# Two gate and up units of the first tile computed ahead of the first flag, as fp32 products

## The reference

```python
# attn: three-tap convolutions, norm, linear attention with rotation, gate, MLP of 1024
x = x + dwconv(x); shortcut = x; xn = ln(x)
act_res = silu(xn @ actp_w + actp_b)
xi = silu(dwconv(xn @ in_w + in_b))
...
x = shortcut + attn * act_res @ out_w + out_b
...
# ffn: ternary weights (-1, 0, 1), scaled per row
h = silu((xn @ w1.T) * w1_s) * ((xn @ w2.T) * w2_s)     # 256 -> 1024: gate and up
h = gelu((h @ h1.T) * h1_s); h = gelu((h @ h2.T) * h2_s)
return (h @ w3.T) * w3_s
```

## Time and profile before

| | us |
|---|---|
| median of 3 runs (lowest, highest) | 1061.14 (1061.04, 1061.63) |
| the profiled execution | 1058.51 |
| its span, first to last instruction | 1056.7 |
| TensorE busy in the span | 1015.6 (96%) |
| VectorE, ScalarE, POOL busy | 760.4 (72%), 602.3 (57%), 237.4 (22%) |

### The profile page before, as it was taken

How to read it: one execution, slowest core, us unless ns; L and a number is a source line. 1 busy time by engine, 2 the same in 40 slices (tenths; PEclk the granted TensorE clock), 3 DMA queues, 4 the chain that set the end, 5 groups by cost and what they waited for, 6 DMA issues and landing times. The chain is left out here.

```text
span 1056.7 us, 17178 instructions
## 1 busy us (share of the span) xinstructions
PE 1015.6 (96%) x6628; PEld 907.1 (86%) x6628; DVE 760.4 (72%) x964; ACT 602.3 (57%) x875; POOL 237.4 (22%) x214
## 2 busy tenths in 40 slices
PE   3999999999999999999999999999999999999998
PEld 3778777888877778888888989989999999999998
DVE  6874689534548579988888466966878967776664
ACT  4788667676444364565555535556556654665444
POOL 3454255224305111111110120231200211101100
PEclk9999999999999999999999999999999999999999
DMA  8989614966784635524312673234493423222310
GB/s 308 408 252 387 201 61 153 330 206 209 282 285 162 195 119 199 180 81 142 118 60 81 228 271 118 81 100 143 155 381 148 152 81 121 91 75 83 113 41 22
DMA packets 68258, 180.15 MB, mean 170 GB/s; under 512 B 5024, under 2 KB 26144, under 8 KB 64544
## 3 DMA queue, kind: packets, MB, share of 16 engines
q1 hardware_dynamic: 68176, 179.03, 48.9%
HBM read 121.34 MB, written 66.06 MB: 177 GB/s over the span
## 5 line engine op out<-in xcount | busy, mean ns | idle before, releaser
L2278 PE MATMUL pr<-xp_hi,wb 128*128 128x256 f32 x1344 | 320.2, 282 | 1.3 <-DVE u L2012 1.1
L2278 PE MATMUL pr<-xp_lo,wb 128*128 128x256 f32 x1344 | 319.6, 281 | 0.0
L2278 PEld LDWEIGHTS pr<-xp_hi,wb 128*128 128x128 f32 x1344 | 255.3, 190 | 3.2 <-issue 3.2
L2278 PEld LDWEIGHTS pr<-xp_lo,wb 128*128 128x128 f32 x1344 | 255.8, 190 | 0.0
L2278 PE MATMUL pr<-u_hi,ring 128*128 128x512 f32 x256 | 102.3, 400 | 3.0 <-issue 1.1
L2278 PE MATMUL pr<-u_lo,ring 128*128 128x512 f32 x256 | 100.0, 391 | 0.0
L1426 ACT CAST xp_hi<-tf 128x1024 fp32r<-128x1024 f32 x48 | 50.2, 1046 | 57.3 <-PE pr L2278 19.9
L1056 POOL TENSOR_TENSOR ot<-ot,yg 128x512 f32<-128x512 f32 x14 | 25.2, 1805 | 244.5 <-DVE ot L2057 244.5
L2466 PE MATMUL pr<-wf_hi,h_hi 128*128 128x256 f32 x256 | 75.5, 295 | 0.6 <-DVE h_lo L1865 0.6
L2006 DVE TENSOR_TENSOR xp_lo<-tf,xp_hi 128x1024 fp32r<-128x1024 f32 x48 | 60.8, 1266 | 20.2 <-ACT xp_hi L1426 20.1
L2466 PE MATMUL pr<-wf_lo,h_hi 128*128 128x256 f32 x256 | 72.1, 281 | 0.0
(11 more groups left out here) (236 smaller groups left out, 2521.7 us busy)
## 6 DMA issues: line engine op xcount, KB each, us to landing
ring<-w_s SPq DMA_DIRECT2D x42, 512.0 KB, 7.3
uf<-h_s SPq DMA_DIRECT2D x16, 1024.0 KB, 5.0
wb<-s_s SPq DMA_DIRECT2D x8, 1024.0 KB, 9.7
wb<-w_s SPq DMA_DIRECT2D x6, 1024.0 KB, 10.9
vw<-v_s SPq DMA_DIRECT2D x8, 514.0 KB, 6.9
xt<-x SPq DMA_DIRECT2D x8, 512.0 KB, 6.0
xn_s<-xh SPq DMA_DIRECT2D x8, 512.0 KB, 9.0
stage<-w_gated SPq DMA_DIRECT2D x2, 2048.0 KB, 13.4
```

Source lines behind the costliest of these rows:

```text
L2278: return e.matmul(bank, w.bitcast(dt), v_.bitcast(dt), start=first, stop=last, skip_group_check=True)
```

## The change

The table gets a place `early` ahead of step -1 with units 0 and 1; `after_back2` of step -1 loses two. The four sums of these units (gate and up, m = 0 and 1) are computed in `opening` as plain fp32 products, straight from the staged piece 0 and `xh[0]`, without a split and without a flag: eight products of 512 columns, two chunks each. One stands before `norm_tokens(0)`, six between it and `norm_back(0)`, one after it. Their silu (ScalarE), gate (VectorE) and the high and low part of `u` for m = 0 move into the opening lists of those engines. The offsets and the bit sum move to `kv_bank`, so that the three banks are free; three quarters of the offsets go ahead of the transposes of tile 1. The ring is filled with pieces 1 to 6 (`filled` counts the fills of a slot). Two half checks no longer stand behind gates 0 and 1 but ahead of the loop. Unit 2 and 3 now stand at `first`, and so on.

```diff
-FRONT_ROOM = [(("p", P1_STEPS[0], "first"), 2, 1), (("p", P1_STEPS[0], "after_a1"), 1, 1),
+FRONT_ROOM = [(("p", P1_STEPS[0], "early"), 2, 0), (("p", P1_STEPS[0], "first"), 2, 1), (("p", P1_STEPS[0], "after_a1"), 1, 1),
               (("p", P1_STEPS[0], "after_a2"), 1, 1),
-              (("p", P1_STEPS[0], "after_back1"), 2, 1), (("p", P1_STEPS[0], "after_back2"), 2, 0)] + \
+              (("p", P1_STEPS[0], "after_back1"), 2, 1), (("p", P1_STEPS[0], "after_back2"), 0, 0)] + \
...
+EARLY = len(FRONT["p", P1_STEPS[0], "early"])
+def filled(piece):
+    return 16 * (piece // RING + int(piece % RING > 0))
@@ SyncE
-                for piece in range(RING):
+                for piece in range(EARLY // 2, EARLY // 2 + RING):
                     sp.wait_ge(staged(piece), 16)
-                    sp.dma_start(ring[:, piece, :].bitcast(F32), stage(piece)).then_inc(s["w_in"][piece], 16)
+                    sp.dma_start(ring[:, piece % RING, :].bitcast(F32), stage(piece)).then_inc(s["w_in"][piece % RING], 16)
...
-                if piece == RING:
+                if piece == RING + 1:
                     sp.wait_ge(s["w_kept"], 16)
...
-            sp.wait_ge(s["gate_mm"], 1)
+            sp.wait_ge(s["gate_mm"], EARLY + 1)
@@ POOL, ahead of the loop over the steps
+            pool.wait_ge(s["up_mm"], EARLY)
+            low_of_u(0)
@@ ScalarE
             def high_of_u(m):
                 e.wait_ge(s["gated"], m + 1)
+                if m < EARLY:
+                    e.wait_ge(s["checked"], FIRST_LAYER + 2)
                 e.copy(u1_hi[:, m, :], full1[:, m % 2, :]).then_inc(s["u_hi"], 1)
...
+            def silu_early(m):
+                e.wait_ge(s["gate_mm"], m + 1)
+                e.activation(silu1[:, m, :], front_bank[bank_use(m) % 3], ACT.Silu, scale=par("w1_s", m)) \
+                    .then_inc(s["silu_d"], 1)
...
             conv1_centre(1)
+            silu_early(0)
             apply_norm(0)
             apply_xn(2)
             high_of_norm(0)
+            silu_early(1)
             copy_xn(2)
             apply_xn(3)
             xi_out(0)
             act_out(0)
+            high_of_u(0)
@@ VectorE
+            def gate_early(m):
+                e.wait_ge(s["up_mm"], m + 1)
+                e.wait_ge(s["silu_d"], m + 1)
+                e.scalar_tensor_tensor(out=full1[:, m, :], in0=front_bank[(bank_use(m) + 1) % 3], scalar=par("w2_s", m),
+                                       in1=silu1[:, m, :], op0=ALU.mult, op1=ALU.mult).then_inc(s["gated"], 1)
...
             check_staged(range(1, 3))
+            gate_early(0)
             low_of_norm(0)
...
-            set_flag(0, front_bank[0][0:1, 0:1])
+            set_flag(0, kv_bank[0:1, 8:9])
+            gate_early(1)
             check_staged(range(4, 6))
             norm_moments(1)
             check_staged(range(6, 7))
+            for m in range(EARLY):
+                check_half(m)
@@ TensorE
+            def early(m, layer, k):
+                if m == 0 and layer == 0 and k == 0:
+                    e.wait_ge(staged(0), 16)
+                    e.wait_ge(s["xh_w"], 1)
+                use = bank_use(m) + layer
+                bank_read(use)
+                w = stage(0).rearrange("p (m w k n) -> p m w k n", m=2, w=2, k=KC)
+                last = e.matmul(front_bank[use % 3], w[:, m, layer, k, :], mid(xh[0])[:, k, :],
+                                start=(k == 0), stop=(k == KC - 1))
+                if k == KC - 1:
+                    last.then_inc(s[("gate_mm", "up_mm")[layer]], 1)
...
             def opening():
                 a_channels(0)
+                offsets_of_weights(0, 1, 2)
                 a_channels(1)
-                offsets_of_weights()
+                offsets_of_weights(3)
+                early(0, 0, 0)
                 norm_tokens(0)
+                early(0, 0, 1)
+                for layer, m in ((1, 0), (0, 1)):
+                    for k in range(KC):
+                        early(m, layer, k)
+                early(1, 1, 0)
                 norm_back(0)
+                early(1, 1, 1)
                 a_channels(2)
                 in_proj(0)
                 e.wait_ge(s["biased"], 1)
-                sum_bits(0, front_bank[0][0:1, 0:1])
+                sum_bits(0, kv_bank[0:1, 8:9])
```

## The result

The changed kernel takes 1062.45 us (median), the kernel before beside it 1061.01: a ratio of 1.0019, 95% interval 1.0010 to 1.0028, so 1.1 to 3.0 us slower. The forecast was 1059.7. The profiled execution took 1063.18 us, span 1061.4, mean granted clock 0.991 (before: 1058.51, 1056.7, 0.998).

The account below looks back on a forecast made before the run. TensorE was taken as the bound nearly everywhere, with VectorE beside it before the second flag. Opening 0, 1.4 us saved before the second flag, nothing given back later: median 1061.14 to 1059.7 us, range 1057.2 to 1062.2.

Parts of the forecast that it names:

- The price of the products: Opening, TensorE: one fp32 product of 512 columns costs 0.86 us at the higher clock level, 1.72 at the lower.
- the offsets into their gap: Opening, TensorE: twelve of sixteen offset instructions, 2.56 us, move into a gap of 2.53 us; cost about 0.05 us.
- `norm_back(0)` under its cover: Opening, TensorE: it ends at 28.0 us, without cost because ScalarE reads it only at 29.15; cover 1.1 us.
- `pb_lo` late: Sign of being wrong in the opening: VectorE's `pb_lo` starts later than the expected 30.2 us.
- products at 0.43 behind the hole: Sign of being wrong on the clock: TensorE products 0.43 us each after the new hole ahead of unit 4.
- From the first flag to the second: Stretch between the flags: TensorE loses 3.7 us of work, VectorE 0.74; hidden unit at 62.35 us, 1.4 us saved.
- gate 2 at 44.2: VectorE between the flags: gate 2 starts at 44.2 us, where VectorE has won 1.2 us and TensorE 4.3.
- 0 for the opening: Sum of the forecast: the opening, up to the first flag, neither saves nor costs time.
- u_lo(0) come after its other work: POOL: the added wait and `u_lo(0)` stand behind its other work; no cost was put down.
- the input projection starts at 31.5 as now: End of the opening, TensorE: the projection waits for `pb_lo` and starts at 31.5 us, unchanged.
- at the higher level: TensorE's input projection runs at the higher clock level from its start and ends some 0.6 us sooner.
- the clock falls in the new hole: Rival, chance 0.08: ahead of unit 4 TensorE idles 2.9 us, units 4 and 5 run at 0.43; 1061.5 us.

Follow-up runs that it names:

- e2: The changed kernel with `u_lo(0)` moved ahead of the inverse deviation of tile 1 on POOL; ratio to the kernel before 1.0004 [0.9991, 1.0016].
- e7: The changed kernel with both reorderings, `u_lo(0)` first on POOL and `gate_early(0)` between VectorE's two checks; 1059.58 us for 1060.88 before, ratio 0.9992.
- e8: e7 with `silu_early(1)` ahead of `apply_xn(2)`, `gate_early(1)` ahead of `pb_lo`, and half checks one behind each gate again; ratio to the kernel before 1.0009.
- e9: e8 plus five dummy fp32 products around the second bit sum, three ahead and two behind; ratio to the kernel before 1.0009 [0.9996, 1.0022].
- e11: e10 plus dummy fp32 products, read by nobody, around the second bit sum; ratio to the kernel before 0.9988 [0.9979, 0.9997].
- e3: The changed kernel with eight dummy products in the opening's holes, five ahead of tile 2's transposes and three behind; ratio to the kernel before 1.0012.
- e4: The changed kernel with `gate_early(0)` moved between VectorE's two staged checks; ratio to the kernel before 0.9998 [0.9986, 1.0009].
- e12: e11 with three dummy products around the second bit sum, two ahead and one behind, in place of five; 1059.36 us for 1061.09 before, ratio 0.9982.
- e6: The changed kernel with eight dummy fp32 products, read by nobody, between units 3 and 4; 1062.21 us, ratio to the kernel before 1.0005.
- e5: The kernel before, unaltered, timed again as if an experiment; ratio to itself 1.0005 [0.9996, 1.0014].
- e10: e8 with `u_lo(1)` also moved ahead of the inverse deviation of tile 1 on POOL; ratio to the kernel before 1.0007 [0.9994, 1.0020].

## Why the prediction was wrong

**What held.** The price of the products, the offsets into their gap, `norm_back(0)` under its cover, the table load on ScalarE, VectorE's gate 2 as what unit 4 waits for, and, from the second flag to 298 us, nothing given back. Two of the prediction's own signs of being wrong came: `pb_lo` late, and products at 0.43 behind the hole.

**The step that failed is "From the first flag to the second": gate 2 at 44.2, and with it the sum's "0 for the opening".** Gate 2 came at 48.46. The 4.26 us come apart by the rows above. Flag 0 is late by 1.71 (38.28 for 36.57); VectorE then waits 0.83 for `norm_tokens(1)`; the half checks begin at 45.46 for 42.82 (1.71 + 0.83, and 0.1 in the list between) and take about what was put down; gate 2 then waits 1.70 for POOL. From gate 2 on the forecast came out nearly right: 18.30 us to the hidden unit for 62.35 − 44.2 = 18.15. Part of that is luck, since two errors offset each other (see the rival below); and the sum had left out the 0.15 us from the end of VectorE's maximum to the bit sum (62.47 and 62.62 in the kernel before).

**1.70 us: "u_lo(0) come after its other work", costed at nothing.** The buffer has two halves, so gate 2 needs the reader of gate 0. In the kernel before that `u_lo` came after the inverse deviation as well, but there gate 0 itself came later, and `u_lo(0)` ended at 44.81, ahead of gate 2 at 45.36. The prediction named the queue and left out who waits for it. e2 settles this.

**2.5 us: "the input projection starts at 31.5 as now" and "at the higher level".** Two failures in a row. `nb_h` was late by 1.16 us because the order of VectorE and POOL turned round; and the hole behind TensorE's last fp32 product, which grew by that, was not looked at at all. TensorE idled 2.10 us, did 1.09 us of transposes, idled 1.11 and then ran all twelve products low: the projection's bit sum came 5.39 us after its start, for 35.07 − 31.51 = 3.56 before. e7, e8, e9 and e11 undo the first and with it the second; e3 shows that products in the holes hold the level. In e4 and e7 to e12 the level held there behind shorter holes (0.77 and 1.11 in e4, 1.09 and 1.10 in e7).

**The rival "the clock falls in the new hole" happened, at its place and with the level it named.** It hardly shows against the forecast (18.30 for 18.15), since the six half checks behind gate 2 took 6.1 us in sum and not the 6.6 put down; no run prices it alone. The same fall in the earlier hole, which no rival had, made the projection 1.8 us longer (5.39 for 3.56). The Trainium skill, "TensorE: Matmul & The Clock Gate", Why this matters for your kernels, warns of idle gaps between bursts; the rows agree in the new hole (3.32 us, then 0.50). Part 4 of that page of the Trainium skill, weighed in the prediction, says that the higher level doesn't engage for transposes; the rows differ: eight took 1.09 us in each of three places of the changed kernel, the first behind a single fp32 product, and 1.95 to 1.97 in the opening of the kernel before.

**What stays open.** By 67 us the trace lost 3.0 us; the two timings show 2.0 and 1.1 (ratios 1.0019 and 1.0010). The level isn't lost in every execution alike: in e6, runs with a mean clock of 0.996 or more took 1058.2 to 1061.9, those below 1062.5 to 1064.8. So the profiled execution may be one of the worse. The kernel before, in e5, shows no such split. How the 2.5 and the 1.7 us share the median wasn't separated beyond e2 and e4, whose intervals overlap.

Behind the first key denominators the fourteen traces take from 761.3 to 765.0 us to the end, whatever their opening (761.6 and 762.9 in the kernel before, 763.3 and 765.0 in the changed one): a spread as large as the effect. Whether the 1.7 us that the changed kernel's trace loses there are of this spread or of the change, no run tells. e12's trace reaches the denominators 0.74 us sooner than the kernel before and still has the longer span (1058.3 for 1056.7). So the traces speak for the opening here, and only the timed runs for the whole.

## What to carry to other kernels

When work moves earlier, go through every buffer that its consumers reuse, and look for the reader that frees it in the queue of the slowest engine: a reader that costs nothing now may stand behind a wait. When work leaves TensorE's stretch, ask what holds its level in each hole that appears or stays, not in the longest alone; and if a few products are put in to hold it, they must end before what they protect is ready.

## What the runs showed of the hardware that was not expected

- A POOL step on four columns (the power aside) takes 0.20 to 0.23 us alone and up to 1.2 where it has to wait for a VectorE check to end: 0.2 us of a lead on VectorE moved a chain of three such steps by 1.16 us. The lead goes with TensorE's faster opening: in all fourteen traces of the table POOL's power took 1.02 us where the opening's transposes took 1.95 or more, and 1.48 to 1.57 where they took 1.85 or less.
- The same opening ran its transposes in 1.09 to 1.97 us in different executions of like code (e2 1.10, e4 1.97): when TensorE's level rises there differs between executions.
- Behind holes of 1.53 us (e2) and 2.72 us (e7) unit 4 kept the higher level; behind holes of 3.32 and 4.51 us it did not.
- The level can fall without a hole. In all fourteen traces it falls once more between 330 and 336 us, while TensorE does 32 products of one column (3.7 to 5.6 us) or just behind them. In the kernel before TensorE doesn't idle there, and the product of 512 columns behind them takes 0.78 us and not 0.47:

```profile
329.77 3.92 PE L2388 MATMUL pr<-prm,wf_raw 128*128 128x1 f32 x32
333.56 0.78 PE L2278 MATMUL pr<-xg_hi,ring 128*128 128x512 f32 x1
```

- In the kernel before, the profile's granted clock reads 1.00 where eight transposes take 1.97 us (26.57) as well as where they take 1.04 (38.10). Its record begins only at 32.8 us, with the first rise, and what lies ahead of it is counted as 1.00. There the level is read from the durations of like instructions.
- From the second flag to the hidden unit 0.79 to 0.84 us pass in the kernel before and the changed kernel, but 1.46 to 1.65 in e7, e8, e10 and e12, put down to "issue". The traces don't show what that is.
